# Flamingo-style block on one core: the contexts' inverse square roots by Newton's iteration on VectorE

## What is computed

```python
def _layer_norm(x, g, b, eps=1e-05):
    mu = jnp.mean(x, axis=-1, keepdims=True)
    var = jnp.mean((x - mu) ** 2, axis=-1, keepdims=True)
    return (x - mu) * jax.lax.rsqrt(var + eps) * g + b
...
q_in = _layer_norm(query_sequences, ln_g, ln_b)
k_in = _layer_norm(key_sequences, ln_g, ln_b)
v_in = _layer_norm(value_sequences, ln_g, ln_b)
q, k, v = (heads(a @ W + b) for ...)          # 16 heads of 64, then _rope(q), _rope(k)
scores = jnp.einsum('bhqd,bhkd->bhqk', q, k) * (1.0 / np.sqrt(D_Q))
scores = jnp.where(valid[:, None, None, :], scores, -jnp.inf)
attn = jax.nn.softmax(scores, axis=-1)
out = jnp.einsum('bhqk,bhkd->bhqd', attn, v)
```

## Time and profile before

| | |
|---|---|
| median of three runs | 2907.51 us (2904.9 to 2911.35) |
| the profiled execution | 2903.99 us |
| its span in the trace | 2901.8 us |
| PE busy | 2618.3 us, 90% |
| DVE busy | 2005.0 us, 69% |
| ACT busy | 1448.7 us, 50% |
| POOL busy | 1387.3 us, 48% |
| mean granted clock of TensorE | 0.949 |

### The profile page before, as it was taken

One profiled execution on the slowest core, in us unless ns is written; L12 is line 12 of the kernel. 1 busy time (PEld: TensorE's weight loads), 2 busy tenths in 40 slices (PEclk: granted clock), 3 DMA queues, 4 the chain that ended last, 5 costly groups with the idle time before them and its releaser, 6 DMA issues. The chain is left out here.

```text
span 2901.8 us, 82200 instructions
## 1 busy us (share of the span) xinstructions
PE 2618.3 (90%) x32664; PEld 1564.2 (54%) x32664; DVE 2005.0 (69%) x6348; ACT 1448.7 (50%) x2248; POOL 1387.3 (48%) x1227
## 2 busy tenths in 40 slices
PE   4679999999988659999999999999999999996598
PEld 3433333333345636666666666666666666664365
DVE  3468888888865667776766767767677667662655
ACT  2247777777755035545446445455464454443122
POOL 2000000000001037887888878878888788885100
PEclk8689999999998869999999999999999999997799
DMA  5521111111100020000000000000000000001000
GB/s 151 152 90 22 26 23 25 22 26 23 25 24 8 22 80 7 19 13 7 19 13 6 18 13 8 24 7 19 13 7 19 13 7 8 7 2 52 0 0 14
DMA packets 109630, 75.20 MB, mean 26 GB/s; under 512 B 43907, under 2 KB 101579, under 8 KB 108752
## 3 DMA queue, kind: packets, MB, share of 16 engines
q1 hardware_dynamic: 109264, 70.08, 8.7%
HBM read 56.61 MB, written 13.43 MB: 24 GB/s over the span
## 5 line engine op out<-in xcount | busy, mean ns | idle before, releaser
L1508 ACT ACTIVATE a_probs<-psS 128x1024 f32<-128x1024 f32 (+1 forms) x448 | 431.4, 963 | 609.8 <-PE psS L1389 606.4
L645 ACT ACTIVATE a_probs<-psS 128x1024 f32<-128x1024 f32 (+2 forms) x512 | 443.2, 866 | 207.7 <-PE psS L586 207.3
L1825 POOL TENSOR_TENSOR a_acc<-a_acc,a_probs 128x512 f32<-128x512 f32 x320 | 407.0, 1272 | 193.4 <-ACT a_probs L1508 183.8
L1412 PE MATMUL psX<-a_probs,a_values 128*64 128x256 f32 x3328 | 443.4, 384 | 0.0
L672 DVE CUSTOM_DVE_ANT_0 a_junk<-psT,a_mask 128x384 f16<-128x384 f32 (+1 forms) x683 | 378.1, 573 | 61.5 <-PE psT L562 41.6
L1827 POOL TENSOR_TENSOR a_acc<-a_acc,a_probs 128x512 f32<-128x512 f32 x320 | 407.0, 1272 | 25.1
L1669 DVE CUSTOM_DVE_ANT_0 a_junk<-psT,a_mask 128x400 f16<-128x400 f32 (+1 forms) x513 | 281.9, 572 | 139.0 <-PE psS L1364 74.1
L1669 DVE CUSTOM_DVE_ANT_0 a_junk<-psS,a_mask 128x400 f16<-128x400 f32 (+1 forms) x511 | 281.2, 572 | 133.5 <-PE psT L1364 73.4
L989 POOL MEMSET r_ones<- 128x128 f16 x1 | 0.2, 205 | 695.2 <-POOLq L719 695.2
L1412 PEld LDWEIGHTS psX<-a_probs,a_values 128*64 128x64 f32 x3328 | 223.6, 137 | 103.4 <-issue 28.8
L1799 POOL TENSOR_TENSOR a_klo<-a_kt,a_khi 128x400 f16<-128x400 f32 (+1 forms) x256 | 242.6, 948 | 18.9 <-ACT a_khi L1560 18.9
(11 more groups left out here) (342 smaller groups left out, 5605.9 us busy)
## 6 DMA issues: line engine op xcount, KB each, us to landing
a_kd<-p_kst SPq DMA_DIRECT2D x24, 416.0 KB, 3.1
a_wq<-in_wq SPq DMA_DIRECT2D x64, 128.0 KB, 2.1
a_keys<-a_kd SPq DMA_DIRECT2D x96, 75.0 KB
p_ctx<-in_ctx SPq DMA_DIRECT2D x8, 768.0 KB
a_ctx<-in_ctx SPq DMA_DIRECT2D x8, 768.0 KB
a_queries<-a_lowest SPq DMA_DIRECT2D x256, 0.5 KB, 2.0
p_mask_raw<-in_mask_t SPq DMA_DIRECT2D x16, 224.0 KB, 4.4
a_queries<-a_qd SPq DMA_DIRECT2D x64, 52.0 KB
```

The source lines that it names most:

```text
L645: nc.scalar.activation(dst, src, ACT.Exp).then_inc(exp_done, 1)
L1412: ins = nc.tensor.matmul(w.sums[n % 2][64 * hd:64 * hd + 64, 0:T], w.values[:, n % 2, c, 64 * hd:64 * hd + 64], w.probs[:, k % RING1, 2 * ...
L1508: nc.scalar.activation(dst, src, ACT.Exp).then_inc(exp_done, 1)
L1825: nc.gpsimd.tensor_tensor(acc, acc, src[:, :, 0, :], ALU.add).then_inc(sum_step, 1)
```

## The change

The step `deviation` on ScalarE goes, and with it the semaphore `ln_root`. `inverse` on VectorE gets the root from `a_var` by a shift and a subtraction of the bit pattern and four Newton steps, in two new tiles of 128 x 13. Every instruction of it is linked to the next by the semaphore `root_step`. The last product goes to `a_rstd`, in place of the reciprocal, and `a_moved` follows as before.

```diff
+ROOT_START, ROOT_STEPS = 0x5F3759DF, 4
...
+        w.root, w.rest = sb("a1_root", [P, SC]), sb("a1_rest", [P, SC])
...
-            def deviation(nb):
-                act.wait_ge(ln_step, 5 * nb + 3)
-                nc.scalar.activation(w.var[:, :], w.var[:, :], ACT.Sqrt).then_inc(ln_root, 1)
-
...
-            deviation(0)
...
-                    if normed_in(it) is not None and sl == 0:
-                        deviation(normed_in(it))
...
+            root, roots_done = chain(dve, root_step)
+
             def inverse(nb):
-                dve.wait_ge(ln_root, nb + 1)
+                dve.wait_ge(ln_step, 5 * nb + 3)
+                bits, guess = w.rest[:, :].bitcast(I32), w.root[:, :].bitcast(I32)
+                root(nc.vector.tensor_scalar(bits, w.var[:, :].bitcast(I32), 1, None, ALU.logical_shift_right))
+                root(nc.vector.tensor_scalar(guess, bits, -1.0, float(ROOT_START), ALU.mult, ALU.add))
+                for i in range(ROOT_STEPS):
+                    root(nc.vector.tensor_tensor(w.rest[:, :], w.root[:, :], w.root[:, :], ALU.mult))
+                    root(nc.vector.tensor_tensor(w.rest[:, :], w.rest[:, :], w.var[:, :], ALU.mult))
+                    root(nc.vector.tensor_scalar(w.rest[:, :], w.rest[:, :], -0.5, 1.5, ALU.mult, ALU.add))
+                    if i < ROOT_STEPS - 1:
+                        root(nc.vector.tensor_tensor(w.root[:, :], w.root[:, :], w.rest[:, :], ALU.mult))
                 if nb > 0:
                     dve.wait_ge(ln_normed, SC * nb)
-                nc.vector.reciprocal(w.rstd[:, :], w.var[:, :]).then_inc(ln_step, 1)
+                nc.vector.tensor_tensor(w.rstd[:, :], w.root[:, :], w.rest[:, :], ALU.mult).then_inc(ln_step, 1)
                 dve.wait_ge(ln_step, 5 * nb + 4)
```

More of the change, by code:

```diff
@@ L1205, in attention1 @@
     loaded, w_loaded, w_hi, w_lo = (s.sem(f"a1_{n}") for n in ("loaded", "w_loaded", "w_hi", "w_lo"))
-    ctx_ready, ln_step, ln_root, ln_normed = (s.sem(f"a1_{n}") for n in ("ctx_ready", "ln_step", "ln_root", "ln_normed"))
+    ctx_ready, ln_step, root_step, ln_normed = (s.sem(f"a1_{n}") for n in ("ctx_ready", "ln_step", "root_step", "ln_normed"))
     c_hi, c_lo, x_full, x_taken = (s.sem(f"a1_{n}") for n in ("c_hi", "c_lo", "x_full", "x_taken"))
```

## The result

| | before | after |
|---|---|---|
| median of six runs each | 2905.24 us (2903.03 to 2911.35) | 2935.88 us (2931.68 to 2942.59) |
| the profiled execution | 2903.99 us | 2931.68 us |
| its span | 2901.8 us | 2929.7 us |

The changed kernel takes 1.0104 times as long (95% interval 1.0089 to 1.0119), 30.6 us more by the medians and 27.7 by the profiled executions. The forecast was 24.2 us more on the profiled execution and 2931 as a median; the measured median lies 5 us above that, inside the range. The profiled execution of the changed kernel is the fastest of its six, so what follows accounts for 27.7 us and leaves some 3 us of the medians' difference aside.

The account below looks back on a forecast made before the run. ScalarE's queue was taken to bound the norm pairs: slot 1's exponent waits for a_moved, normalise and a table load. 15.5 + 5.7 + 3 = 24.2 us on 2903.99 gave 2928.2, as a median 2931; range 2917 to 2944.

Parts of the forecast that it names:

- The loads: ScalarE, behind normalise in seven norm pairs: each removed Exp load gives back 1.29 us; Sqrt loads and roots count nothing.
- The chain: VectorE, norm pairs: 18 linked instructions at 0.21 us make a_moved 3.51 us later, net 2.22 us a pair, 15.5 in seven.
- the rival of a cheap chain: Norm pairs: links at 0.075 us each, so the kernel is not slower, +2 us, 2909.5; 6 in 100.
- GpSimd's port: Norm pairs: the chain finds GpSimd idle, nothing added; as a rival, GpSimd takes the port, 6.7 us more, 8 in 100.
- The first context: Ahead of the loop: the chain meets three GpSimd instructions, is blocked by them, and a_moved comes 5.7 us later.
- The clock: TensorE's granted clock in norm pairs: four cheap pairs may turn costly, 0 to 6 us; half taken, 3 us.
- the rival of more frequent falls: Norm pairs and pairs behind: the clock falls more often than taken, 3 us more, 2934; 10 in 100.

Follow-up runs that it names:

- e1: The kernel before with the square root left out, so both table loads and the root are gone and nothing is added: 2890.72 us, 0.995 of before.
- e2: The changed kernel with two Newton steps in place of four, 10 linked instructions in place of 18: 2912.6 us, 1.0024 of before.
- e7: The changed kernel with two Newton steps and fused instructions, 7 linked instructions in place of 18: 2909.64 us, 1.0022 of before.
- e5: The changed kernel with normalise one slot later on ScalarE, so slot 1's exponent no longer stands behind it: 2938.15 us, 1.0112 of before.
- e10: The changed kernel with GpSimd's split of the weights waiting until the first context's a_moved is there: 2932.78 us, 1.0084 of before.
- e6: The kernel before, square root and reciprocal kept, with normalise one slot later on ScalarE: 2891.93 us, 0.9938 of before.
- e9: The changed kernel with 7 links spread over slots 2 to 5, normalise wholly in the next pair, GpSimd's weights split later: 2876.43 us, 0.9897 of before.
- e3: The changed kernel with TensorE repeating slot 0's products three more times in slot 1 of each norm pair: 2921.56 us, 1.006 of before.

## Why the prediction was right, and where it was not

**The loads.** Right. Of eight Exp loads at the exponent's line one is left, the loop's own:

```profile
L1510 ACT ACT_TABLE_LOAD  x1: 1283/1283/1283, 1096.0 to 1096.0; - x1
```

Each gave back more than the 1.29 us of the forecast: from the start of `normalise` to that of the exponent it took 1144.58 - 1142.39 = 2.19 us and takes 1151.23 - 1150.44 = 0.79, so 1.40 came back; e1, which only removes, shows 1.41. The exponent now starts 0.09 us before `normalise` ends, which the load had prevented. The Trainium skill (ScalarE: Activation LUTs, section "What ACT_TABLE_LOAD costs") states such an overlap of about 93 ns for ACTIVATEs in a row, and the trace agrees. Its 2.66 us for a switch does not show here.

**The chain.** Right: 0.208 us a link against 0.21, and `a_moved` later by 3.48 us (1150.40 - 1142.60 against 1142.35 - 1138.03) against 3.51. Net per norm pair 3.48 - 1.40 = 2.08 against 2.22, in seven 14.5 us against 15.5. One reading of the prediction is off without touching the sum: a norm pair's 3.99 us more than an ordinary one are not all between slots 0 and 1, where it is 6.55 against 2.19, 4.36 more; the gap behind, 2.17 against 2.51, gives a part back. e2 and e7 confirm the price by length, and the rival of a cheap chain falls; its break-even of 0.087 us a link was less than half of what a link takes.

**GpSimd's port.** As forecast, it held nothing in the norm pairs: all 128x13 links there take 0.17 us. The margin was 0.07 us, and e5 shows what lies behind it: links of 1.1 us.

**The first context.** Right, +5.6 us against 5.7 (the prediction's own terms, 1039.1 - 1033.46, give 5.6 too), two links blocked as described. e10 takes the blocking away and shortens this stretch by 3.7 us; the prediction had put 3.8 on it.

**The clock.** This is the step that failed, by its size: "0 to 4 x 1.5 = 6 us. I take half, 3 us" in the norm pairs measured 11.5. The prediction took a costly fall at the 1.59 us that one costs before and counted only how many pairs would have one. All seven have one, as at its upper bound. In the first two norm pairs the price held, 1.5 us each. In the five others it is 2.5 to 2.7: there the clock stands low in one piece, for 6.8 us instead of the 3.4 of a costly fall in before, and at the end of a standstill of TensorE that is longer than any the prediction looked at. It gave the second standstill 2.9 us, from the first pair's 0.70. In the first two norm pairs it is 2.72 and 2.92. In the five without a covered fall it is 4.1 to 4.3, where before's four pairs without one stood for 2.21. Of before's three costly falls one came behind slot 2's scores, one while they ran and one as they started (2.16, 2.47 and 3.01 us from slot 1 to 2); after, the clock falls as they start in six of the seven (2.98), and slot 2 to 3 takes up to 5.54.

At the same time pair 24, which is no norm pair, lost the costly fall that it had in before's profile, -2.0 us (slot 5 to 6 took 10.05 us at a granted clock of 0.83 and takes 8.02 at 1.00). The prediction has nothing of it. The runs do not show what decides: e6, which keeps the root, has the fall too, while e1, with neither root nor chain, is without it, and so is every run with Newton's steps. So the chain is not needed to lose it.

The sum came out as 14.5 + 5.6 + 11.5 - 2.0, less 1.5 for the earlier start and 0.4 of the rest, 27.7 us, where the prediction had 24.2. That it was so near is luck in part: the clock's term was 8.5 us too low, and 5.0 us came off elsewhere, 3.5 of them from pair 24 and the earlier start, which no term foresaw. By the medians the forecast was 6.4 us too low. The clock's term had the right sign; the rival of more frequent falls, 3 us more on top of the 3, had the right mechanism but stopped at 6.

**What stays open.** Why the clock's first fall comes in some norm pairs and not in others is not shown. In the change it comes in the first two pairs, which lose 1.5 us each; in e10, with the same code in the loop, it comes in the first alone, which loses 2.8 all the same, after a standstill of 2.78 us. So the longer standstill goes with the higher price in the change, but that it sets the price is not shown. Nor was before tried with `normalise` wholly in the next pair, so how much of e9's 31 us needs the chain in place of the root is open; e6, the nearest of that kind, is 15 us slower than e9.

## What to carry to other kernels

A sequence of small linked instructions is priced by its count (0.21 us each here); 18 of them in place of a root, a reciprocal and two table loads lose, seven break even. What decides here is less the price than the queue that the sequence stands in: the same seven links spread over slots in which nobody waits for them, with `normalise` moved behind them, make the kernel 31 us faster than before. When a wait in front of TensorE grows, add to it what the granted clock does behind it, taken from a stretch with a wait of the new length, not of the old, and check it after: with seven links the wait was shorter than before and the clock cost more.

## What the runs showed of the hardware

What the granted clock costs does not follow from the gap between the exponents alone. With a gap of 6.55 us (before) a norm pair lost 0 or some 1.5 us; with 8.6 us (the change) 1.5 or 2.5 to 2.7; with 6.32 us (e7) 1.6 to 1.9 in all seven, with 6.95 (e2) 0 or 1.3 to 1.6. TensorE's standstill ahead of slot 2's scores does not tell it alone either: of the four pairs of before that stood for 2.21 us three lost some 1.5 us and one nothing, all seven of e7, which stood for 1.96 us, lost 1.6 to 1.9, and the five of the change that stood for 4.1 to 4.3 us lost 2.5 to 2.7. In the change the clock stood at 0.5 for 6.8 us of each norm pair, in before for 3.4 in six of seven. Useless products in TensorE's wait (e3) gave 14.3 us back.

A TENSOR_SCALAR on integers with a single input was held by GpSimd as the two-input links were: 2.04 us ahead of the loop, 0.17 in e10 where GpSimd waited, while the reciprocal of before ran through the same stretch in 0.24 us.
